# Graph layer with routed experts: per-accumulator clear counts, eight table scatters in flight, routing and experts in one block

## The reference, cut to what matters

```python
# x: 12500 x 256; src, dst: 212500 edges (sorted by dst); edge_weight: 212500
xn  = layernorm(x)
gnn = segment_sum(edge_weight[:, None] * (xn @ weight_l)[dst], src) + bias_l + xn @ weight_r + bias_r
mix = (linear attention over all rows of xn, times a gate from xn) @ Wproj + bproj
x   = x + gnn + mix
z   = layernorm(layernorm(x)) * gamma + beta
w   = softmax of the top 2 of 8 router logits (z @ Wr + br), zero elsewhere
x   = x + sum over the 8 experts e of (gelu(z @ W1[e] + b1[e]) @ W2[e] + b2[e]) * w[:, e]
```

## Time and profile before

| | us |
|---|---|
| median of 3 runs | 4441.68 |
| lowest and highest of the runs | 4427.51 to 4441.93 |
| the profiled execution, its own time | 4410.35 |
| span of the profiled execution | 4408.4 |
| setup and clears, up to the first scatter | 152.5 |
| edge phase from there | some 3,100 |
| routing | some 363 |
| experts | some 790 |

### The profile page before, as it was taken

The page is one execution under the profiler, slowest core; times in us unless marked ns, Lnnn a source line. Parts: engine busy times, 40 slices in busy tenths (PEclk is TensorE's granted clock), DMA queues, the critical chain, the costliest instruction groups (busy, mean ns, idle before and its releaser), DMA issues. The chain is left out here.

```text
span 4408.4 us, 85937 instructions
## 1 busy us (share of the span) xinstructions
PE 3387.8 (77%) x16649; PEld 2799.6 (64%) x16650; DVE 2647.6 (60%) x11867; ACT 1660.1 (38%) x3046; POOL 3117.6 (71%) x2089
## 2 busy tenths in 40 slices
PE   1467666666676767788888878888768869999999
PEld 1355555555555555666666666666557758888888
DVE  3577777665565555666666666666547764444444
ACT  1233333244444443444444444444311113333333
POOL 0588888888888888888888888888855554444444
PEclk7788788787888888888888888888879989999999
DMA  8889888877777777777777777777779866666665
GB/s 364 260 162 174 170 159 170 170 123 116 116 109 117 116 107 114 108 108 104 106 108 108 101 108 108 103 106 109 92 178 274 253 204 142 138 143 142 141 141 116
DMA packets 573617, 637.99 MB, mean 145 GB/s; under 512 B 59217, under 2 KB 534251, under 8 KB 571857
## 3 DMA queue, kind: packets, MB, share of 16 engines
q0 software_dynamic: 279264, 270.04, 49.3%
q1 hardware_dynamic: 246752, 260.61, 20.0%
q10 hardware_dynamic: 47504, 106.29, 6.3%
HBM read 248.34 MB, written 390.31 MB: 145 GB/s over the span
## 5 line engine op out<-in xcount | busy, mean ns | idle before, releaser
L849 POOL DMA_INDIRECT agg<-msg,sidx x1664 | 2584.0, 1553 | 661.9 <-issue 408.5
L1153 PE MATMUL bank<-rows,Cmat 128*128 x3328 | 1026.6, 450 | 166.4 <-ACT msg L1346 141.4
L1346 ACT COPY msg<-bank 128x512 f32<-128x512 f32 x832 | 487.1, 585 | 1477.3 <-DMA agg<-msg,sidx 1211.2
L1153 PEld LDWEIGHTS bank<-rows,Cmat 128*128 128x128 f32 x3328 | 699.8, 225 | 347.8 <-issue 254.6
L904 DVE SCALAR_TENSOR_TENSOR sidx<-seen_sum,trash,srcf 128x4 int32<-128x4 f32 x416 | 92.7, 223 | 1018.1 <-DMA agg<-msg,sidx 1011.7
L2169 POOL DMA_INDIRECT out_dram<-x_y,x_node x210 | 334.4, 1592 | 456.9 <-DVE x_y L2137 376.4
L887 DVE TENSOR_SCALAR Emat<-bank,srcf,wtf 128x128 f32<-128x128 f32 x1664 | 565.5, 401 | 0.0
L1137 PEld LDWEIGHTS bank<-Emat,pick 128*128 128x128 f32 x3328 | 514.1, 225 | 40.6 <-issue 16.2
L1128 PE MATMUL bank<-packed,both 128*128 (+1 forms) x416 | 185.9, 447 | 446.0 <-DVE seen L891 427.1
L1137 PE MATMUL bank<-Emat,pick 128*128 128x128 f32 x3328 | 525.2, 310 | 1.7 <-DVE seen L891 1.7
L891 DVE SCALAR_TENSOR_TENSOR seen<-bank,srcf,prior 128x128 f32<-128x128 f32 x1664 | 480.8, 345 | 0.0
(11 more groups left out here) (260 smaller groups left out, 4311.6 us busy)
## 6 DMA issues: line engine op xcount, KB each, us to landing
x_w<-in_L_ffn_W_dram SPq DMA_DIRECT2D x105, 512.0 KB, 4.4
agg<-expert_rows ACTq DMA_DIRECT2D x12, 4224.0 KB, 58.7
r_agg<-agg SPq DMA_DIRECT2D x196, 256.0 KB
x_rows<-expert_rows_table SPq DMA_DIRECT2D x105, 261.0 KB, 4.6
window_raw<-in_x_dram SPq DMA_DIRECT2D x208, 128.0 KB, 2.5
agg<-msg,sidx POOLq DMA_INDIRECT x1664, 3.8
xn_rows<-n_xn ACTq DMA_DIRECT2D x49, 256.0 KB
xn_turned<-n_xnT ACTq DMA_DIRECT2D x49, 256.0 KB
```

What stands on the lines that cost most here:

```text
L849: pool.indirect_dma_start(scratch["agg"][r][:, :], bass.IndirectOffsetOnAxis(ap=sidx[:, j:j + 1], axis=0), msg[:, j % (2 * BATCH), :], Non ...
L1153: mm = nc.tensor.matmul(M[p][:, (q % 2) * D:(q % 2 + 1) * D], Cmat[:, b % 2, q, :], rows[:, bass.ds(slot, 1), :], start=True, stop=True)
L1346: nc.scalar.copy(msg[:, at:at + 2, :].rearrange("p q c -> p (q c)"), M[p][:, :]).then_inc(s_msg, 1)
```

## The change

It has three parts.

1. **Setup and first group.** `s_zeroed` becomes four semaphores, one for each accumulator. ScalarE's wait for the 11 weights ahead of the first 7 clears is removed, and SyncE issues the weights in another order, small ones first. VectorE's and TensorE's waits for all 11 weights stay. In group 0 the chunks go to the accumulators in the order `FIRST_GROUP` (agg3 first at the eighth chunk), and each accumulator's first chunk waits for that accumulator's clears alone. All later waits on `s_add` are shifted by `SHIFT`. The steps for the first pairs of `x` tiles move to later places of group 0.
2. **Routing.** The scatters count into eight semaphores, by the parity of the pair, so each waits for the one two pairs before; `r_pos` gets 8 slots.
3. **One block for routing and experts.** The end of the routing block goes. SyncE waits for the plan, loads W1 of the first two expert blocks, waits for fills and scatters (`table_complete`) and then loads table rows; the other engines wait for the plan (`s_plan`) where they first read it. The fills write two neighbouring rows from each partition instead of rows 128 apart. `xe` and `y` of the expert phase lie in the buffer of the routing's `xin`.

```diff
-        s_zeroed = sem("accumulators_cleared")
+        s_zeroed = [sem(f"accumulator_cleared{r}") for r in range(NACC)]
...
-        weights = [(mix["wq"][:], ...), (mix["wk"][:], ...),
+        weights = [(mix["bg1"][:], row(t["L0_mix_bg1"])),
+                   (mix["brows"][:, 0, :], ...), (mix["brows"][:, 1, :], ...), (mix["brows"][:, 2, :], ...),
+                   (mix["wg1"][:], ...), (mix["wq"][:], ...), (mix["wg2"][:], ...), (mix["wk"][:], ...),
                    (mix["wv"][:], ...), (mix["wproj"][:], ...),
...
             act.wait_ge(s_clear, 5)
-            act.wait_ge(s_w, WEIGHTS)
-            act.nop(nofuse=True)
-            for acc, n in clears[:READY]:
-                act.dma_start(clear_rows(acc, n), zeros).then_inc(s_zeroed, 16)
+            for r, n in clears[:READY]:
+                act.dma_start(clear_rows(scratch["agg"][r], n), zeros).then_inc(s_zeroed[r], 16)
...
+FIRST_GROUP = (0, 1, 2, 0, 1, 2, 0, 3) + 2 * tuple(range(NACC))
+SHIFT = tuple(FIRST_GROUP.count(r) - len(FIRST_GROUP) // NACC for r in range(NACC))
...
-                    if not (first(g) and b == 0):
-                        pool.wait_ge(s_add[r], 16 * (NB * g + b))
+                    if first(g):
+                        r = FIRST_GROUP[j]
+                        if r not in FIRST_GROUP[:j]:
+                            pool.wait_ge(s_zeroed[r], 16 * CLEARS)
+                        else:
+                            pool.wait_ge(s_add[r], 16 * FIRST_GROUP[:j].count(r))
+                    else:
+                        pool.wait_ge(s_add[r], 16 * (NB * g + b + SHIFT[r]))
...
-            pool.wait_ge(s_zeroed, 16 * NACC * CLEARS)
...
-                steps = [(2 + u, lambda u=u: statistics(n, u)) for u in pairs_of(n)]
-                steps += [(10 + u, lambda u=u: normalise(n, u)) for u in pairs_of(n)]
+                steps = [((10 if first(n) else 2) + u, lambda u=u: statistics(n, u)) for u in pairs_of(n)]
+                steps += [((14 if first(n) else 10) + u, lambda u=u: normalise(n, u)) for u in pairs_of(n)]
...   (TensorE's turn and keys, and ScalarE's copies of them: place 15 in group 0)
-        pos = sb("r_pos", [P, 2, 2, 2], I32)
+    pos = sb("r_pos", [P, TURN, 2, 2], I32)
-        s_sent = [[sem(f"r_sent{c}{m}") for m in range(2)] for c in range(2)]
+    s_sent = [[[sem(f"r_sent{s}{c}{m}") for m in range(2)] for c in range(2)] for s in range(2)]
...
-                        if not below(i, 1):
-                            pool.wait_ge(s_sent[c][m], 16 * i)
+                    if not below(i, 2):
+                        pool.wait_ge(s_sent[u % 2][c][m], 16 * turns_before(i, u))
...
-                if not below(i, 2):
+            if not below(i, TURN):
-                            dve.wait_ge(s_sent[c][m], 16 * (i - 1))
+                        dve.wait_ge(s_sent[u % 2][c][m], 16 * turns_before(i - TURN, u) + 16)
...
-                engine.dma_start(scratch["table"][bass.ds(at, CAP), :].rearrange("(a p) d -> p a d", p=P),
+            engine.dma_start(scratch["table"][bass.ds(at, CAP), :].rearrange("(p a) d -> p a d", p=P),
                                  fill[:]).then_inc(s_filled[half], 16)
-            engine.wait_ge(s_filled[half], 16 * NE // 2)
...
-        block = ctx.enter_context(nc.Block(no_gpsimd_drain=True))
...
+        sp.wait_ge(s_plan, PLANNED)
+        for q in range(2):
+            load_weights(q, q)
+        table_complete(sp)
             for u in range(AHEAD):
                 load_rows(0, u)
```

More of the change, by code:

```diff
@@ L69 @@
 DEPTH = 4
+PLANNED = 23
 TURN = 2 * DEPTH
@@ new lines, in body @@
+        def body(i, u):
+            old = None if below(i, 2) else (i - 2, (u - 2) % TURN)
+            if old:
+                route(*old)
+            gather_sums(i, u)
+            statistics(i, u)
+            if not (isinstance(i, int) and i >= PAIRS - 2):
+                add_halves(i + 2, (u + 2) % TURN)
+            scale(i, u)
+            if old:
+                position(*old)
+        add_halves(0, 0)
+        add_halves(1, 1)
+        over_turns(dve, body)
+        for i in range(PAIRS - 2, PAIRS):
+            route(i, i % TURN)
+            position(i, i % TURN)
@@ new lines, in rank, with body @@
+                    mm = nc.tensor.matmul(total, onesb[:], hot[:, c, m, :], start=(c == 0 and m == 0),
+                                          stop=(c == 1 and m == 1))
+            mm.then_inc(s_rank, 1)
+        def body(i, u):
+            if not below(i, 1):
+                turn(i - 1, (u - 1) % TURN)
+            if not (isinstance(i, int) and i == PAIRS - 1):
+                weigh(i + 1, (u + 1) % TURN)
+            if not below(i, 2):
+                rank(i - 2, (u - 2) % TURN)
+            if not below(i, 1):
+                logits(i - 1, (u - 1) % TURN)
+            if not (isinstance(i, int) and i >= PAIRS - 2):
+                sum_turned(i + 2, (u + 2) % TURN)
```

1207 lines of the change are left out of this document (601 added, 606 removed).

## The result

The changed kernel takes 4598.05 us (median of 6 runs, 4592.65 to 4604.38) against 4441.31 for the kernel before (6 runs, 4427.51 to 4445.77). The ratio is 1.0349, with a 95% interval of 1.0336 to 1.0363. It is slower by 3.5%, some 156 us, where 0.6% faster was forecast. That lies outside the forecast range of 4388 to 4442 us, and beyond the 4479 us of rival C, the slow case, too. The profiled execution has a span of 4596.4 us.

A forecast was written before the change was run, and what follows sets the result against it. GpSimd's scatters were taken to bound the edge phase, TensorE the experts, no full engine routing. Terms -1 - 20 - 5 = -26 us took 4441.7 to 4416 us, own range 4400 to 4434; 4388 to 4442 reaches into rivals A and B.

The forecast's parts named there:

- rival C: Routing: with eight scatters in flight accumulator loads come late and VectorE waits for them; +37 us, 4479 us; chance 0.07.
- What bounds the kernel now: Whole kernel by stage: DMA limits the clears, GpSimd the edge scatters at 1.85 us each, TensorE the experts; routing none.
- The shifted counts in the later groups: Edge phase after group 0: the shifted waits ask for the same scatters as before, 0 us.
- Part 1: Clears and first group: weights starve behind clears, first scatter at 150 us instead of 152.5; -1 us, bounds -16 and +12.
- Rival A: Setup: the weights do not starve, the last clear lands at 139.2 us; -51 us in all, 4391 us; chance 0.23.
- the late engine: Setup: one DMA engine with 53 weight packets left behind clears, 1.12 us each; weights land at about 83 instead of 25.8 us.
- the moved steps: Group 0: steps meet at places 14 and 15 and group 1's x rows load later; 2 us taken for it.
- Part 2: Routing: VectorE's 20.1 us wait at its write of r_pos goes, 6.2 us a pair; -20 us, bounds -27 and -6.
- B: Routing: the DMA takes VectorE's place as limit, part 2 gives -6, in all -12, 4430 us; chance 0.18.
- the bound of -6: Routing: smallest gain of part 2, if the DMA is not fit for more than a share of about 0.93.
- Part 3: Seam from routing to experts: row loads follow the fills at once, W1 is there; -5 us, between -1 and -8.

The follow-up runs named there:

- after: The changed kernel with all three parts, against the kernel before: 4598.05 us, ratio 1.0349.
- strict_only: The kernel before with only VectorE's wait at batch 0 of a group made stricter for agg3, as the change does it: 4592.78 us, ratio 1.0331.
- balanced: exact with each load of 31 edge-list rows cut into 16 and 15 rows: 4422.59 us, ratio 0.9947 against the kernel before.
- exact: The changed kernel with the batch 0 wait put right, VectorE's group 1 taken out of its loop: 4441.21 us, ratio 0.9998 against the kernel before.
- base_again: The kernel before, unchanged, profiled in a second execution: span 4441.1 us, routing 7.29 us a pair.
- bal_unrolled: balanced with four scatters' rival left aside: all 49 routing pairs written out without a loop, eight in flight; ratio 0.9958 against the kernel before.

## Why the prediction was wrong, point by point

**What bounds the kernel now: right, and the key to the result.** "The end of the edge phase moves with the time at which the first scatters can go, and with nothing else" held for every run but two, if it is taken from the ninth scatter, behind which no clear is waited for: from there to the last scatter eleven executions take 3080 to 3089 us, after and strict_only 3237 and 3235. In those two, GpSimd's gaps are no longer 0.30 us throughout. The sentence is true only as long as messages are there in time, and the row on the messages, 19.7 us in 58 places before, had been left unread.

**The step that failed: "The shifted counts in the later groups wait for the same scatters as before: 0."** It was stated for all batches and holds for three in four. The count has `max(SHIFT[r], 0)` at batch 0. I took what the shift means for what the code does, and never put r = 3, b = 0 into the line. Doing so gives 16 x (nb - 3) where 16 x (nb - 4) belongs: one batch, 7.4 us, stricter, in each of 103 groups. The price was in sight as well. VectorE waited at that line in 389 places of 416 in the kernel before (L904, us and times):

```profile
  DMA agg<-msg,sidx: 1011.7, 389
```

A line where an engine waits nearly every time is where it has just as much lead as the wait gives it, and a stricter wait there takes lead away. A bound of 0 to 103 x 7.4 = 762 us would have been due; 154 us of that came, as strict_only shows (3251.7 against 3097.6). The rest VectorE seems to work off where it has less to do: between 1750 and 1950 us of the changed kernel GpSimd waits for messages 5.4 us in 7 places, from 600 to 800 us 30.7 us in 17, and in the kernel before VectorE is busy 122.4 us and 144.8 us of these stretches. That is argued, no run varied it.

**Part 1, the mechanism: right; the sum: near.** These are the steps as forecast and as the changed kernel has them:

| | forecast | after |
|---|---|---|
| VectorE's copy of the small vectors | 83 | 85.7 |
| second clears issued | 96 | 98.5 |
| setup ends | 106 | 103.5 |
| second window at VectorE | 137 | 134.0 |
| first scatter | 150 | 148.0 |
| ninth scatter | 165 to 168 | 168.5 |

The rows of it are these, first the setup:

```profile
85.70 0.17 DVE L358 COPY mix_columns<-bank 128x6 f32<-128x6 f32 x1 [45.37 <-issue]
...
103.50 0.60 ACT L286 COPY wqT<-bank 128x512 f32<-128x512 f32 x1
...
133.96 0.43 DVE L967 BATCH_NORM_STATS2 window_stat<-window_raw 128x6 f32<-128x256 f32 x1 [9.42 <-DMA window_raw<-in_x_dram]
```

and the two queues from 30 to 60 us, with a packet of one for a packet of the other, as the earlier trace rows had it:

```profile
q10 hardware_dynamic: 416, 12.44, 96.0%
q1 hardware_dynamic: 416, 0.39, 3.8%
```

Rival A falls. That the sum came out so near is in part luck, for two errors have opposite signs: VectorE's copy comes 2.7 us later than forecast, and from it to the end of setup it takes 17.8 us (85.70 to 103.50), where 23.2 were taken over from the kernel before.

The Trainium skill's rule ("DMA: Bandwidth & Descriptors", section on queues, rings and completion order), that an engine drains some 9 to 17 descriptors before it changes queues, does not describe these loads: in the kernel before, each of the three stretches of 1.29 us from 94 us on holds 16 packets of either queue, as many as there are engines. The prediction's estimate from that rule, that the weights would land before 39.7 us, also took a clear's packet as a single piece. With 9 to 17 pieces in it, at the 1.12 us of the earlier trace rows for each, five such packets would take 50 us or more, an estimate with that page's figure, and the rule would not have spoken for rival A. The Trainium skill, on the same page in the section on why a DMA increments its semaphore by 16, does describe why one engine was late: a copy runs on the largest number of engines, up to 16, that divides the slowest dimension of both its sides. For 31 rows that is one engine, for 16 rows and 15 rows it is 16 and 15. The trace agrees for the 31 rows, with the 6% of the earlier trace rows.

The prediction had seen the late engine but not asked what made it late, and balanced shows that this was the larger matter: 19 us below the kernel before, where the change as it was meant (exact) is level with it.

One term was mis-sized. For the moved steps I took 2 us. In exact, two gaps appear behind the first batches that the kernel before has not, 6.27 us instead of 1.85 at 179.72 us and 3.39 at 194.21. That is 6 us. Up to the ninth scatter part 1 is 1.5 us ahead (167.89 in exact against 169.41), and at the last it is 2.5 to 3.5 us behind (3253.6 against 3251.1 and 3250.1).

**Part 2: wrong.** "That wait ... is gone. ... So nearly all can be had: -20 us" rested on one execution. The wait was 6.3 us in the next, and with it gone (after has none for scatters) VectorE's other waits are there as in base_again (24.3 and 14.3 us for these two):

```profile
DVE r_place L1762 <- remote: 28.3, 20, 4.0
DVE r_place L1762 <- PE bank L1902: 15.6, 9, 3.3
```

Measured was 7.46 us a pair, not 6.2, and 7.29 in base_again. Neither is B right, since the DMA share fell to 0.75 over the stage, nor C, since VectorE waits 5.5 us in 2 places for `r_agg` in after and 5.4 in 2 in base_again. No engine is full there; what is left is the chain of VectorE, TensorE and ScalarE with its pauses. The prediction had noted that its execution was 31 us under the median and carried the difference over unasked. Where those 31 us lay was the question that would have corrected part 2. One more figure has no run behind it: that the DMA is not fit for more than a share of about 0.93, behind the bound of -6. From 94 to 113 us its two queues add up to more than that the earlier trace rows.

**Part 3: right, its size about half.** The first expert matmul comes 19.4 us after the last write of `r_pos` (18 forecast, 22.9 before). Over all executions the seven with one block have 19.4 to 22.1 us, 20.5 in the mean, and the six with two blocks 21.9 to 23.4, 22.7 in the mean. That is -2 to -3 us for -5. The terms did not give -5 either: their middles add up to some -4, and their ends to -7 and -1. The chain around it, which answers to the earlier trace rows:

```profile
3806.36 1.60 SPq L2037 DMA_DIRECT2D x_w<-in_L_ffn_W_dram  x2
3809.50 3.80 SPq L2029 DMA_DIRECT2D x_rows<-expert_rows_table  x4
...
3816.35 5.34 PE L2084 MATMUL bank<-x_xf,x_w 128*128 128x256 f32 x16 [1.20 <-ACT x_xf L2109]
```

W1 is no longer waited for. But both W1 loads are issued 4.7 us after the last scatter, ahead of the rows, which start at 3809.50, 7.8 us behind the last scatter's issue (3801.66); before it was 6.5 (3614.42 to 3620.94), in base_again 8.9. In after and the first execution of before the gain lies in the last scatters: the last is issued 4.8 us after the last write of `r_pos` (3796.9 to 3801.66), where it was 9.7 us (3604.7 to 3614.42). Over all executions it lies mostly behind them: from the last scatter to the first expert matmul it is 13.8 us in the mean with one block and 15.3 with two, from the last write of `r_pos` to the last scatter 6.7 and 7.5.

**The third rival.** C was to be the case on the slow side, with 0.07. It had the wrong place. The rival that was missing belongs to every change that rewrites the counts of waits: one count is too high, and only the time tells.

## What to carry to other kernels

Put numbers into every changed semaphore count, for the first and the last value of each index, and compare which transfer each one waits for. A count that is too high costs a lead, which is dear where the line waited nearly every time already. Before a wait is priced, read it in a second execution, above all when the profiled one lies away from the median. And when one DMA engine is late, look for a small load with an awkward number of rows: on top of the change, cutting 31 rows into 16 and 15 was worth 23 us, where the three parts by themselves were worth nothing that can be told.

## What the runs showed of the hardware

- Four loads of 31 rows left one DMA engine late: 99 + 46 packets left on it from 18 to 26 us; with each load cut into 16 and 15 rows, 5 of SyncE's are left (balanced). That cost 50 us of start (85.7 against 35.8 us for VectorE's copy) once clears stood behind it.
- Where two queues have packets of 1 KB and of 33 KB for the same engines, they go one for one, a pair in 1.29 us (94 to 95.29 us of the kernel before: 16 and 16 packets).
- Beside clears an accumulating scatter of 128 rows lands about 11 us after the one before it (what waits for them goes at 124.94 and 135.96 us in balanced); without clears they are issued every 1.85 us. By the earlier trace rows a packet costs 1.12 us there, and 128 / 16 = 8 rows on each engine would make 9.0 us, an estimate of the same size.
- The same program routes at 6.64 us a pair in one execution and 7.29 in another. In the first ScalarE's copies of the turned sums all follow TensorE's result, in the other three start 1.8 to 4.1 us after it, with no releaser in the trace. The one that was followed up (bal_unrolled) comes 4.1 us late, with a granted clock of 0.50 behind it. Such copies stay with the loop written out; their cause is open.
- At both passes from one turn of eight pairs to the next VectorE idles 4.5 to 6.1 us with no releaser (before, base_again, balanced). With turns of four pairs no such piece is over 0.8 us, and with the loop written out it is 0.3 us.
